# One guest instead of two between the gate and up products of a macaron block

## What is computed

```
gate = xt @ Wg.T ; up = xt @ Wu.T
inter = gelu_tanh(gate) * up
ffn = inter @ Wd.T
att = softmax(causal(q @ k.T / 4)) @ v
x = x + 0.5 * ffn(layernorm(x))
x = x + (att of layernorm(x)) @ w_out.T
x = x + 0.5 * ffn(layernorm(x))
```

## Time and profile before

| | |
|---|---|
| median of 3 runs | 1003.79 us (1000.8 to 1006.43) |
| the profiled execution | 1007.13 us, span 1005.3 us |
| TensorE busy | 931.5 us (93%), granted clock 0.983 in the mean |
| VectorE busy | 620.5 us (62%) |
| ScalarE busy | 469.0 us (47%) |
| GpSimd busy | 232.7 us (23%) |
| chain that ended last | PE 76%, DVE 8%, ACT 6%, issue 6% |

### The profile page before, as it was taken

One profiled execution on the slowest core, in us unless ns is written; L12 is line 12 of the kernel. 1 busy time (PEld: TensorE's weight loads), 2 busy tenths in 40 slices (PEclk: granted clock), 3 DMA queues, 4 the chain that ended last, 5 costly groups with the idle time before them and its releaser, 6 DMA issues.

```text
span 1005.3 us, 16744 instructions
## 1 busy us (share of the span) xinstructions
PE 931.5 (93%) x6726; PEld 409.1 (41%) x6726; DVE 620.5 (62%) x1015; ACT 469.0 (47%) x634; POOL 232.7 (23%) x261
## 2 busy tenths in 40 slices
PE   2779999999998999988999999999999998999998
PEld 1335554544444544322544422234442222345544
DVE  6976344665877777677778867768786451252221
ACT  1324043123227332487433189873309999733240
POOL 4645076134200431000333000004300000052240
PEclk9889999999999999899999999999999999999999
DMA  8000015007000060000042000000000000000000
GB/s 258 1 0 2 1 42 63 1 2 105 1 2 2 2 105 1 1 2 2 2 80 26 21 2 2 2 2 1 1 1 22 2 2 2 1 1 1 22 1 21
DMA packets 21803, 20.26 MB, mean 20 GB/s; under 512 B 4064, under 2 KB 21472, under 8 KB 21728
## 3 DMA queue, kind: packets, MB, share of 16 engines
q1 hardware_dynamic: 18528, 16.06, 8.6%
q10 hardware_dynamic: 3200, 3.15, 1.0%
HBM read 12.78 MB, written 6.29 MB: 19 GB/s over the span
## 4 chain that ended last, share of the span: by engine, by line
PE 76%; DVE 8%; ACT 6%; issue 6%; DMA 2%; POOL 1%; SPq 1%; ACTq 0%; DVEq 0%; POOLq 0%
PE ps L1119 12%; PE ps L1090 11%; PE ps L1091 11%; PE ps L1092 11%; PE ps L1268 8%; PE ps L1223 7%; ACT inter L733 6%; PE ps L1120 6%; PE ps L1251 4%; DVE sg L1031 2%; DVE sg L1028 1%; DVE oT L819 1%; PE ps L1235 1%; PE ps L1194 1%; DMA qreg<-qk_split 1%
## 5 line engine op out<-in xcount | busy, mean ns | idle before, releaser
L733 ACT ACTIVATE inter<-ps 128x1024 f32<-128x1024 f32 (+3 forms) x320 | 265.9, 898 | 34.9 <-PE ps L1235 19.5
L639 POOL TENSOR_TENSOR inter<-wreg,inter 128x512 f16<-128x512 f32 x112 | 129.4, 1158 | 644.7 <-ACT inter L722 644.5
L1031 DVE TENSOR_REDUCE sg<-ps 128x2 f32<-128x1024 f32 (+3 forms) x217 | 220.3, 1037 | 49.2 <-PE ps L1235 24.1
L743 ACT ACTIVATE wreg<-ps,gelu_in 128x512 f32<-128x512 f32 x112 | 77.1, 689 | 270.3 <-PE ps L1092 270.2
L1119 PE MATMUL ps<-wd,inter 128*128 128x512 f16 x512 | 170.8, 380 | 0.0
L895 DVE SCALAR_TENSOR_TENSOR wreg<-ps,kappa,wreg 128x512 f32<-128x512 f32 x128 | 95.7, 748 | 107.9 <-PE ps L1092 102.0
L1028 DVE TENSOR_REDUCE sg<-ps 128x1 f32<-128x512 f32 (+3 forms) x206 | 120.8, 632 | 64.7 <-PE ps L1223 43.7
L1268 PE MATMUL ps<-inter,v 128*17 128x512 f32 (+3 forms) x1280 | 150.1, 541 | 0.7
L1120 PE MATMUL ps<-wd,inter 128*128 128x256 f16 x512 | 139.6, 273 | 0.0
L1223 PE MATMUL ps<-kreg,qreg 48*128 48x512 f16 (+3 forms) x640 | 109.5, 355 | 18.5 <-DVE sg L1031 11.6
L1251 PE MATMUL ps<-qreg,kreg 50*128 50x512 f16 (+3 forms) x640 | 110.4, 355 | 16.2 <-ACT inter L733 10.6
(11 more groups left out here) (136 smaller groups left out, 899.4 us busy)
## 6 DMA issues: line engine op xcount, KB each, us to landing
qk_split<-oT SPq DMA_DIRECT2D x4, 1024.0 KB, 4.5
kreg<-qk_split SPq DMA_DIRECT2D x24, 128.0 KB, 4.8
qreg<-qk_split SPq DMA_DIRECT2D x24, 128.0 KB, 8.5
xres<-in_L_attn_x ACTq DMA_DIRECT2D x4, 512.0 KB, 9.1
out_x<-xres SPq DMA_DIRECT2D x4, 512.0 KB, 2.9
kreg<-in_L_ffn_up_W_packed ACTq DMA_DIRECT2D x4, 256.0 KB, 5.7
kreg<-in_L_ffn_gate_W_packed SPq DMA_DIRECT2D x4, 256.0 KB, 6.9
kreg<-in_L_ffn_down_W_packed SPq DMA_DIRECT2D x1, 1024.0 KB, 9.5
```

The costliest lines, as they stand in the source:

```text
L639: pool.tensor_tensor(inter[:, 1, u, :], prod_ring[:, u % 3, :], inter[:, 0, u, :], ALU.subtract).then_inc(s_inter, 1)
L733: act.activation(p_ring[:, pair % 8, :, 0:w], ps[:, 512 * b:512 * b + 1024].rearrange("p (a q) -> p a q", a=2)[:, :, 0:w], ACT.Exp, scale= ...
L1031: dve.tensor_reduce(m_part[:, r, part, col:col + 9:8], both[:, :, 0:width], AX.X, ALU.max).then_inc(s_slot_read, 1)
```

## The change

`fill_ffn` puts at most one counted item, not two, at each place between the entries of a feed-forward stage. The count covers maxima and all the other listed work but `negate`, `statistics` and `rows`. Everything behind that place in the list is worked out anew by the same planner, in attention stages too, since units that were not taken are still due.

```
             def fill_ffn():
 
                 done = 0
-                while done < 2:
+                while done < 1:
                     for queue in (chain, project_in, todo):
                         if queue and start_of(queue[-1]) <= pe + 0.05 and (queue[-1][0] != "max" or dve <= pe + 2.0):
                             done += queue[-1][0] not in ("negate", "statistics", "rows")
                             put(queue.pop())
                             break
                     else:
                         return
```

## The result

| | before | changed |
|---|---|---|
| median | 1004.54 us (1000.8 to 1006.43, 4 runs) | 1022.08 us (1020.07 to 1023.51, 4 runs) |
| ratio | | 1.0178 (1.0141 to 1.0215) |
| profiled execution, span | 1007.13, 1005.3 us | 1020.75, 1019.0 us |

A forecast was written before the change was run, and what follows sets the result against it. TensorE was taken to bound the feed-forward stages and ScalarE attention 3. Terms -4.0 + 5.5 + 8.6 + 4.3 = +14.4 us, against the median 1003.79, gave 1018 us, range 1006 to 1028.

The forecast's parts named there:

- Feed-forward stages, -4.0: Feed-forward stages: 31 units leaving save 6.1 us, 21 more changes of tiling cost 2.1; sum -4.0 us.
- The price of a change of tiling, 0.10 us: TensorE in feed-forward stages: each change of tiling costs about 0.10 us, +2.1 us for 21; 0.17 if draining each matmul's record.
- Its cover is nothing: Feed-forward stages: nothing hides the -4.0 us, TensorE being the bound.
- Attention 0 to 2, +5.5: Attention 0, 1 and 2 get 1, 2 and 7 more units, costing 0.3, 1.2 and 4.0 us.
- The slope of 1.07 us per guest: Attention 0 to 2: upper bound per added maxima unit, from groups 5 to 7 against 9 to 11.
- Groups 12 to 14, +8.6: Attention 3: from 37 to 58 units in 48 steps, losing 0.18 us a step, 8.6 us.
- The start of group 15, +4.3: Before group 15's first scores: the last unit's reductions, `negate`, `rows`, copy and DMAs are exposed, +4.3 us.
- The clock falls in the new wait: Rival, chance 0.27: TensorE's clock falls in the wait before group 15, about +1 us, 1019 us in all.
- VectorE sets the pace: Rival, chance 0.14: VectorE's reductions limit attention 3, losing 18.2 us instead of 8.6; 1028 us in all.
- Attention has room: Rival, chance 0.12: spread maxima units stay free in attention, only lower bounds count; +2.4 us, 1006 us in all.
- The row hides: Rival, chance 0.05: ScalarE's backlog at the border of groups 14 and 15 hides the wait; -1.9 us, 1002 us.
- What would show it: Signs: feed-forward some 4 us shorter, groups 12-14 31-32 us each, 9-11 some 24.5, line 1223 waits, DMA-ended gap 4-5 us.

The follow-up runs named there:

- experiment 2: Kernel before, at most one maxima unit per place in feed-forward stages, same number per stage, 46 changes of tiling more: 1025.79 us, ratio 1.0209.
- experiment 11: Kernel before, a second maxima unit in a feed-forward place moved to the next place if empty, 26 changes of tiling more: 1012.13 us.
- experiment 5: Kernel before, every second maxima unit of attention 3 moved from between the score pairs to behind the same step's values: 1016.34 us.
- experiment 4: Kernel before, both maxima reductions reading only the first half of each bank: 994.37 us.
- experiment 10: Changed kernel, every maxima reduction reading only an eighth of its columns: 1000.05 us.
- experiment 1: Changed kernel, planner counting 8 places fewer until group 15, so its row of maxima comes earlier: 1014.67 us, 1.0098 of the kernel before.
- experiment 3: Changed kernel, both maxima reductions reading only the first half of each bank: 1006.71 us.
- experiment 6: Changed kernel, attention's maxima units behind the values moved to between the next step's score pairs: 1036.62 us, ratio 1.0335.
- experiment 9: Kernel before, three planner numbers changed (banks free within 0.65 us, VectorE 3 us behind, group 15 counted 6 places early): 1002.41 us, ratio 0.9972.

## Why the prediction was right

The time (1022.1 for 1018) and the sign were right, and so were the parts of the mechanism: shorter feed-forward stages, close guests that cost ScalarE time, and a wait in front of group 15. That the sum came so near was partly luck. In the profiled executions the feed-forward stages came 3.6 us under their term, attention 0 to 2 came 3.3 us under theirs, and groups 12 to 14 5.4 us over theirs. The forecast sum was 14.4 and the measured one 13.7. A part of each of these errors is the clock, and the medians differ by 17.5.

- **Feed-forward stages, -4.0: measured -7.6.** The price of a change of tiling, 0.10 us, held nearly: 0.10 and 0.13 in experiments 2 and 11, where the 0.17 of a drain to the end of each matmul's record would have made 22 changes 3.7 us instead of 2.8. The Trainium skill (TensorEngine Tiling, Key Properties) says that a change of mode drains TensorE; these runs agree that a change costs something, and show the smaller price. What the step left out are the clock and a wait. The products of stage 1 took 57.3 us before and 54.9 now, 2.4 less; experiment 5, which has the order of the kernel before in that stage and no fall of the clock, took 54.9 too. In stage 5 TensorE stood still 0.8 us (56.20 less 55.41 in the earlier trace rows, now nothing), when the transpose of the next inputs (line 1194) waited for a guest's reduction. Less these two, -4.4 is left. "Its cover is nothing" was right, but TensorE wasn't the bound at every moment.
- **Attention 0 to 2, +5.5: measured +2.2.** Attention 0 and 2 came at 0.4 and 5.5, forecast 0.3 and 4.0. Experiment 11, with the order of the kernel before in attention 2 and no fall of the clock, took 94.1 us there, so the change's own cost is nearer 6.9: this term was too small. Attention 1, +1.2 forecast, went to -3.7. Its group 4, in the kernel before at a clock of 0.82, is 2.2 us shorter with more guests and no fall. In experiment 2, with the same order as before and half as long a fall, it took 16.2 us too, so this much is the clock. Groups 5 to 7, with 32 guests for 33, are 1.4 shorter; no run tells why. The slope of 1.07 us per guest, taken between groups 5 to 7 and 9 to 11, had no clock fall in it but compared different placements.
- **Groups 12 to 14, +8.6: measured 14.** 18.5 less the 4.5 us of the wait. This is the term that was most mis-sized: a price per step from the average number of guests, 0.18 at 1.21. By the steps, most of it goes by how close one guest follows another. The changed list puts guests behind the values in one step and between the scores in the next, and so 21 of the 58 guests of attention 3 (none of 37 before) and 31 of the 62 of attention 2 (17 of 55) follow another at a distance of one score pair. Experiment 5 has 0.8 guests a step and still loses 10.8 us; by the average it should have lost none. Not all of the 14 is the guests' distance. Group 12 with the order of the kernel before took 29.6 us, and 31.1 with a fall of 3.4 us (experiments 4 and 11, 1.5 us more); its fall here was twice as long, so by an estimate from these 3 us of the 14 are the clock. Of the other 11, experiment 10 leaves about 5 with VectorE hardly reading, so that about 6 are its reading.
- **The start of group 15, +4.3: measured 4.5.** The step with the wait takes 5.63 us, against 1.09 before and 1.09 in experiment 1. Chain, releaser and price were as forecast.
- **The rivals.** "The clock falls in the new wait" came true beside the forecast: it fell at 852.7, inside the wait, for 6.8 us, group 15 had 0.90, and took 1.1 us more, where +1 was the price. It fell in or right behind this wait in all four kernels that have it (the changed one, experiments 3, 6 and 10), and at that border in none of the ten others. The Trainium skill, TensorE: Matmul & The Clock Gate (Why this matters for your kernels), warns of idle gaps between bursts of matmuls, after which the clock is back at half; the trace agrees, with 4.2 us of idle TensorE between 849.1 and 853.5, broken only by one small transpose. The falls at 417.2 and 577.6 came without such a gap. "VectorE sets the pace" was half right: 14 (11 without the clock) lies between its 18.2 and the 8.6, and VectorE's reading is what a close guest waits for, but VectorE is busy 70.0 of 136.3 us and sets no pace. "Attention has room" is true of single guests (1.82 us a step with one, 1.89 without), and false of close ones. "The row hides" is refuted by 5.16 us of idle ScalarE.
- **What would show it.** Feed-forward shorter by 4 (7.6), groups 12 to 14 at 31 to 32 each (35.0, 33.7, and 32.8 without the wait), waits of line 1223 for 1028 (20.2 us), groups 9 to 11 at 24.5 (25.5), a gap of 4 to 5 us ended by the DMA (5.06): right in kind, and too small in three of five.

## What to carry to other kernels

The cost of filler work in a stage with another bound isn't read from its average number per step alone. It depends above all on the distance from one piece to the next, compared with the time until its buffer is free again: here 0.4 us of matmuls and 1.2 us of reading, with three banks of which a guest takes two. (No run tried a fourth bank.) Before you compare stages of two traces, look up in which of them the clock fell. And before thinning out work in one stage, ask at what distance the planner will set it down in the next, and whether the last piece has a chain (reductions, a transpose, a DMA) behind it that now ends in front of its consumer.

## What the runs showed of the hardware

- The clock was at half for 3.4, 6.8 or 10.2 us at the start of attention stages, in some kernels and not in others with the same order there: head group 12 took 29.6 us in the kernel before, and 31.1 in experiment 11, whose clock fell at 760.8 for 3.4 us. A difference of 1 to 3 us in such a group says little of an edit. In two of the falls of the kernel before, 417.2 and 577.6, TensorE had only stood still in pieces of under 1 us.
- The same order in the products of feed-forward 1 took 54.9, 57.3 and 59.3 us with the clock at half for 0, 3.4 and 6.8 us (experiment 5, the kernel before, experiment 9). The executions of a kernel differ by this too: of 17 of the kernel before, the shortest took 1000.6 us at a mean granted clock of 0.989, the longest 1006.7 at 0.982.
- A reduction in one instruction over two banks takes 1.22 us, two instructions 0.69 each; the second form can release its first bank earlier, and the waits fit that: the longest of guests for line 1031 are 1.6 us, for line 1028 1.1. No run tried one form against the other. (In attention stages the kernel uses two instructions for banks 5 and 6 and for 7 and 5, one for 6 and 7.)
- An eighth of the elements (128x64 for 128x512) still takes 0.22 us of 0.69.
